# Layer 1's token shift: blended rows projected once, in place of two projections

## The reference

```python
shifted = jnp.pad(hidden, ((0, 0), (1, 0), (0, 0)))[:, :-1]
k_in = hidden * time_mix_key + shifted * (1 - time_mix_key)
v_in = hidden * time_mix_value + shifted * (1 - time_mix_value)
r_in = hidden * time_mix_receptance + shifted * (1 - time_mix_receptance)
k = k_in @ Wk
v = v_in @ Wv
r = jax.nn.sigmoid(r_in @ Wr)
rwkv = _wkv(time_decay, time_first, k, v)   # a scan over the 512 tokens
return r * rwkv @ Wo
```

## Time and profile before

| | us |
|---|---|
| median of 3 runs | 2878.58 (2871.51 to 2892.12) |
| the profiled execution | 2878.1 |
| its span, first to last instruction | 2876.1 |
| granted TensorE clock, mean share of full speed | 0.976 |

### The profile page before, as it was taken

How to read it: one execution, slowest core, us unless ns; L and a number is a source line. 1 busy time by engine, 2 the same in 40 slices (tenths; PEclk the granted TensorE clock), 3 DMA queues, 4 the chain that set the end, 5 groups by cost and what they waited for, 6 DMA issues and landing times. The chain is left out here.

```text
span 2876.1 us, 53577 instructions
## 1 busy us (share of the span) xinstructions
PE 2699.7 (94%) x17974; PEld 1985.7 (69%) x17974; DVE 2295.8 (80%) x4760; ACT 2019.7 (70%) x4630; POOL 725.7 (25%) x709
## 2 busy tenths in 40 slices
PE   6999898999999999999696999999999999999997
PEld 4777675566666577777474777777777777777776
DVE  5988886556656656566685999999999999999997
ACT  3556554645546454453384899999999999999997
POOL 2211101101101100000342333334343433333342
PEclk9999999999999999999898999999999999999999
DMA  2000001000000000000401223223232323223221
GB/s 61 2 5 16 30 16 56 1 1 1 1 1 1 1 1 1 1 1 1 123 1 39 54 67 80 54 64 82 63 82 63 81 64 81 57 64 84 52 52 45
DMA packets 79763, 111.56 MB, mean 39 GB/s; under 512 B 16197, under 2 KB 32776, under 8 KB 79496
## 3 DMA queue, kind: packets, MB, share of 16 engines
q1 hardware_dynamic: 75522, 105.77, 15.1%
q10 hardware_dynamic: 3974, 2.37, 0.3%
HBM read 34.43 MB, written 6.55 MB: 14 GB/s over the span
## 5 line engine op out<-in xcount | busy, mean ns | idle before, releaser
L75 PE MATMUL banks<-lower 128*128 128x128 f32 (+2 forms) x2688 | 480.4, 359 | 1.4 <-DMA lower<-in_L_w2T 0.8
L75 PEld LDWEIGHTS banks<-lower 128*128 128x128 f32 (+1 forms) x2688 | 316.7, 198 | 162.7 <-issue 161.9
L79 PE MATMUL banks<-ident,scratch 128*128 128x128 f32 x2432 | 397.9, 274 | 17.6 <-DVE scratch L83 12.7
L3343 DVE CUSTOM_DVE_ANT_0 scratch<-scratch,tb,coef 128x512 f32<-128x512 f32 (+3 forms) x512 | 399.2, 815 | 0.8 <-ACT scratch L3428 0.8
L79 PEld LDWEIGHTS banks<-ident,scratch 128*128 128x128 f32 x2432 | 293.8, 142 | 118.8 <-issue 102.5
L75 PE MATMUL banks<-scratch 128*128 128x256 f32 (+3 forms) x1088 | 356.0, 432 | 8.9 <-ACT scratch L3024 8.9
L75 PEld LDWEIGHTS banks<-n,pt 128*128 128x128 f32 x2560 | 310.9, 192 | 56.2 <-ACT pt L3450 43.6
L75 PE MATMUL banks<-n,pt 128*128 128x128 f32 x2560 | 344.5, 278 | 4.4 <-ACT moe L3469 4.3
L83 DVE SCALAR_TENSOR_TENSOR scratch<-scratch,tb 128x512 f32<-128x512 f32 (+3 forms) x512 | 344.7, 693 | 0.0
L3514 POOL TENSOR_TENSOR normed<-normed,aT 128x512 f32<-128x512 f32 x128 | 174.0, 1359 | 570.2 <-DVE normed L3304 485.1
L3438 ACT ACTIVATE scratch<-scratch,mn 128x512 f32<-128x512 f32 (+3 forms) x512 | 285.4, 564 | 0.0
(11 more groups left out here) (432 smaller groups left out, 5137.6 us busy)
## 6 DMA issues: line engine op xcount, KB each, us to landing
scratch<-normed SPq DMA_DIRECT2D x512, 128.0 KB, 2.4
tb<-head_rows SPq DMA_DIRECT2D x16, 512.0 KB, 7.5
tb<-head_rows SPq DMA_DIRECT2D x32, 256.0 KB, 7.2
turn<-head_turns SPq DMA_DIRECT2D x32, 128.0 KB, 3.5
xs<-in_x SPq DMA_DIRECT2D x8, 256.0 KB
head_turns<-loads SPq DMA_DIRECT2D x8, 256.0 KB, 2.5
head_turns<-rotation SPq DMA_DIRECT2D x8, 256.0 KB, 2.5
w<-in_L_Wqk SPq DMA_DIRECT2D x8, 256.0 KB, 3.2
```

The lines of the kernel that those rows point to most:

```text
L75: return self.T.matmul(out, lhsT, rhs, start=start, stop=stop, skip_group_check=True)
L79: return self.T.matmul(out, in_, self.ident[0:n, 0:n], start=start, stop=True, is_transpose=True, skip_group_check=True)
L3343: x = V.tensor_tensor_reduce(y, y, view(hd["tb"][:, e, 2, i * P + 127:i * P + 128], [[-1, n]]), k.coef[:, h:h + 1], 3e38, ALU.add, ALU.min ...
```

## The change

`rw_now` and `rw_before` are no longer made: the plain weights `rw` are kept into layer 1. For each projection ScalarE writes (1 - time_mix) times the shifted rows into one of two buffers (the halves of `hT`), VectorE adds time_mix times the rows, in place, and TensorE multiplies the blend once by the plain weight. The six blends of a chunk go through the two buffers in the order of `BLENDS`; a copy waits until the projection two turns before has been done. The key projection of the second sequence goes one slot later on TensorE, from -3 to -2. The prologue's list loses its six weight scalings, so that all later steps of it move six places forward. The counts `l0_prod` and `l0_back` of layer 0 are used again, with a base.

```diff
@@ ahead_dve
         k.made_step(k.ts(k.rest[:, :], k.rp[:, 2:5], -1.0, 1.0, ALU.mult, ALU.add))
         yield
-        for i in range(3):
-            k.made_step(k.ts(k.rw_now[:, i, :], k.rw[:, i, :], k.rp[:, 2 + i:3 + i]))
-            yield
         k.next_made()
-        for i in range(3):
-            k.made_step(k.ts(k.rw_before[:, i, :], k.rw[:, i, :], k.rest[:, i:i + 1]))
-            yield
@@ layer1_prepare
+        k.l1_past, k.l1_blend = k.l0_prod.again(), k.l0_back.again()
+        k.blend = [k.hT[:, j * S:(j + 1) * S] for j in range(2)]
@@
+    BLENDS = ((1, 0), (0, 0), (0, 1), (1, 1), (2, 0), (2, 1))
+
+    def l1_blend_of(self, i, c, b):
+        return 6 * c + self.BLENDS.index((i, b))
@@ l1_pe
         def project(i, c, b):
-            k.l1_emptied_of(T, b, "open", c, b)
-            if c < 2:
-                T.wait_ge(k.pool.sem, k.l1_made)
-            to = take(b)
-            k.mm(to, k.rw_now[:, i, :], k.nT1[c % 2][:, b, 1:1 + S], stop=False)
-            filled(k.mm(to, k.rw_before[:, i, :], k.nT1[c % 2][:, b, 0:S], start=False), b, i, c, b)
+            n = k.l1_blend_of(i, c, b)
+            k.after(T, k.l1_blend, n + 1)
+            filled(k.mm(take(b), k.rw[:, i, :], k.blend[n % 2]), b, i, c, b)
@@
-            for c in due(-3):
+            for c in due(-2):
                 project(0, c, 1)
@@ l1_dve
+        def blend(i, c, b):
+            n = k.l1_blend_of(i, c, b)
+            k.l1_emptied_of(V, b, "open", c, b)
+            k.after(V, k.l1_past, n + 1)
+            k.stt(k.blend[n % 2], k.nT1[c % 2][:, b, 1:1 + S], k.rp[:, 2 + i:3 + i], k.blend[n % 2],
+                  ALU.mult, ALU.add).then_inc(*k.l1_blend.up())
@@
         for s, due in k.l1_slots():
+            for c in due(-7):
+                blend(1, c, 0)
+            for c in due(-5):
+                blend(0, c, 0)
+            for c in due(-3):
+                blend(0, c, 1)
+            for c in due(0):
+                blend(1, c, 1)
+            for c in due(6):
+                blend(2, c, 0)
+            for c in due(7):
+                blend(2, c, 1)
@@ l1_act
+        def past(i, c, b):
+            n = k.l1_blend_of(i, c, b)
+            k.l1_emptied_of(A, b, "open", c, b)
+            if c < 2:
+                A.wait_ge(k.pool.sem, k.l1_made)
+            if n >= 2:
+                c0, (i0, b0) = (n - 2) // 6, k.BLENDS[(n - 2) % 6]
+                k.l1_filled_by(A, b0, i0, c0, b0)
+            A.activation(k.blend[n % 2], k.nT1[c % 2][:, b, 0:S], ACT.Identity,
+                         scale=k.rest[:, i:i + 1]).then_inc(*k.l1_past.up())
@@
             for c in due(-7):
                 open_copy(c, 0)
+                past(1, c, 0)
             if 0 <= s - 2 < k.UNITS1:
                 silu(s - 2, 1)
+            for c in due(-5):
+                past(0, c, 0)
+            for c in due(0):
+                past(1, c, 1)
+            for c in due(6):
+                past(2, c, 0)
+            for c in due(7):
+                past(2, c, 1)
...
             for c in due(-3):
                 open_copy(c, 1)
+                past(0, c, 1)
```

More of the change, by code:

```diff
@@ L169, in ahead_layer1 @@
         k.rwo, k.rp, k.td = k.sb("rwo", [D, D]), k.sb("rp", [D, 5]), k.sb("td", [D, 1])
-        k.rw_now, k.rw_before = k.sb("rw_now", [D, 3, D]), k.sb("rw_before", [D, 3, D])
+        k.rw, k.rw_before, k.rest = k.sb("rw", [D, 3, D]), k.sb("rw_before", [D, 3, D]), k.sb("rest", [D, 3])
     def ahead_layer3(self):
         k = self
-        k.rw, k.rest = k.sb("rw", [D, 3, D]), k.sb("rest", [D, 3])
         k.noise = k.sb("noise", [D, 2, D])
@@ L1904, in layer2_prepare @@
             k.gv2.append(row[:, 0:B * 72].rearrange("p (b a h c) -> p b a h c", b=B, a=4, h=2))
-        k.pool2 = k.shaped(k.rw_now.rearrange("p i d -> p (i d)")[:, 0:B * 128], (B, 2, 64))
+        k.pool2 = k.shaped(k.rw.rearrange("p i d -> p (i d)")[:, 0:B * 128], (B, 2, 64))
         small = k.rw_before.rearrange("p i d -> p (i d)")
```

## The result

The changed kernel takes 2842.88 us (median of 6 runs, 2834.84 to 2852.71), the kernel before beside it 2886.97 us (6 runs). The ratio is 0.9862, with a 95% interval of 0.9844 to 0.9880: 1.4% faster, where 0.6% had been forecast and the range ended at 2848. The profiled execution took 2836.55 us with a span of 2834.9, against 2878.1 and 2876.1 before.

A forecast was written before the change was run, and what follows sets the result against it. TensorE was taken to set layer 1's pace; -18.1 - 1.0 + 0 + 1.1 + 0.5 = -17.5 us gave a predicted 2861 us (-0.6%), chance 0.62, range 2848 to 2880 (within: 0.91).

The forecast's parts named there:

- What leaves TensorE in layer 1, and its cover: Layer 1: 21 second products of 0.86 us leave, 18.1 us saved; added copies (16.3 us) and blends (16.6 us) stay hidden.
- the slack of the experts' chain: Layer 1 slots: 3.5 us between `up` halves, 1.4 filled, 2.1 left; a blend and the shorter projection leave 0.5 us.
- Rival (a): Layer 1: TensorE reaches each projection before its blend, 1.57 us each, net +17 us: 2895, slower; chance 0.06.
- Rival (c): Layer 1: freed TensorE room is worth nothing, pace set by SiLU and product: 2878 us; chance 0.05.
- The stall near slot 69: Chunk 3, slots 66 to 69: a blend delays VectorE's unbroken run, TensorE waits; 1.1 us lost, bounds 0 and 1.3.
- The start of layer 1: First projections wait for copy, moments and blend, partly at half clock; 0.5 us lost, bounds 0 and 3.
- The blends beside GpSimd: Layer 1: a blend meeting a GpSimd operation could double; expected in two or three of 24, mattering only on slot 67.
- The rest of that list: Layer 0: remaining list steps, including five sines and two logarithms, run two slots earlier; zero, bounds -2.5 and +2.5 us.
- Layer 2 and 3 follow in order behind the experts: Layers 2 and 3: they start as much earlier as layer 1's experts end; no further gain counted.
- Rival (b): Clock: displaced work meets two to four more slowdowns, or layer 1's start takes its 3 us: about 2868; chance 0.15.
- Rival (d): More than counted: layer 0's shift falls well, or a half-speed stretch goes: 2853 us; chance 0.12.
- the 1.0 counted: Prologue: six weight scalings leave VectorE ahead of the first window's maximum; 1.0 us saved, bounds 0 and 1.3.

The follow-up runs named there:

- three empty steps: Changed kernel with three empty steps in the prologue's list, so later steps move forward one slot, not two: 2848.78 us, 0.9880 of the kernel before.
- second profile: Both kernels run and profiled once more, unchanged: kernel before 2884.52 us, ratio 1.0016; changed kernel 2844.41 us, ratio 0.9875.
- the padded one: Kernel before with 80 tiny matmuls (160 instructions) added to TensorE's stream at the start of layer 3: 2872.37 us, 0.9963 of the kernel before.
- the one padded in layer 3: Changed kernel with 48 tiny matmuls (96 instructions) added to TensorE's stream at the start of layer 3: 2852.94 us, 0.9891 of the kernel before.

## Why the prediction was wrong

**What leaves TensorE in layer 1, and its cover: right.** The sum for this layer was -18.1 + 1.1 + 0.5 = -16.5 us. Measured: -18.4 and -15.6 in the two pairs of profiles, and -17.2 in the profile with three empty steps, whose half-speed time (14 us) is the kernel before's. The copy is 0.713 us for 0.68, the blend 0.737 for 0.69, both hidden as argued from the slack of the experts' chain. Doubling the copies cost nothing beyond the clock, doubling the blends 5 us and more of 18: the cover was there, and for the blends it is nearly used up. Rival (a), the exposed hand-over, would have shown in TensorE's waits: of 24 projections only two at the start waited for a blend, 4.3 us together, as the prediction said. Rival (c) falls with the same numbers: what left TensorE left the layer's time, although its weight loads are busy for 285 of 454 us. The rule of the Trainium skill on the weight loads' share ("Perfetto Trace Analysis", Identifying the Most-Contended Engine) would have left room here that was not there.

**The stall near slot 69: right in place, less in size.** 0.72 us for 1.1.

**The start of layer 1: right in order, off by 0.5 to 1 us.** The order came out as worked out: the moments stand ahead of the blend, and the first projection waits for it,

```profile
479.26 2.08 PE L75 MATMUL banks<-hT,rw 128*128 128x512 f32 x2 [3.20 <-DVE hT L83]
```

From the `w1` load's issue (470.84) to the first `up` at 485.62 it is 14.8 us, in the second profile 15.6 and with three empty steps 14.9, where the two profiles before have 15.3 and 15.5: nothing to half a microsecond gained, for 0.5 lost. But the earlier trace rows had the experts' start held back by the landing of `w2`, and I took that for a floor; no wait for DMA is left there: all of the layer, its loads too, starts earlier. A row that names the last to arrive gives a floor only from the issue of that load, not as a fixed time.

**The blends beside GpSimd: did not happen.** Two or three were expected to double. The longest of the 24 took 0.750 us (row above). In the kernel with doubled blends four did meet one, and took 2.49. (Two readings behind the sum were loose, without changing it: the 0.69 us of the earlier trace rows are products of L1480, where the addition of 910.99 has a median of 0.68 in the trace; and 283.51 + 16.6 is 300 and not 301.)

**The failed step: "The rest of that list runs three steps to a slot, thus two slots earlier through layer 0 ... I take zero for all this, bounds -2.5 ... and +2.5."** It was -6.8 us. The bound counted table loads, 1.28 us each. What moved was where TensorE waits: a sine that stood in a slot with a GELU made ScalarE's copy late for the transposes, twice, up to 1.87 us; steps of VectorE's own in another slot made `o` late by 1.5; and 6.8 us of half speed stood behind two of these waits. Idle time is 4.9 of the 7.8 us gained there, the clock 2.9. The first was to be seen before: the chain of the step (copy of L1139 behind L505, with the wait at TensorE). I looked at the one sine of slot 28 and took it for all five. Why the clock fell behind the wait of 1.87 us in the two profiles of the kernel before and not in the padded one stays open.

**The second failed step: "Layer 2 and 3 follow in order behind the experts and start as much earlier."** They did start earlier, and ended earlier still: -5.3 and -11.8 us in layer 2, -7.8 and -10.6 in the heads. In layer 2 the program is the same and the length goes with the time at half speed. The layer by windows in, in order, the changed kernel (422.3 us with 38 at half speed in its two profiles and in the one padded in layer 3), the kernel before (second profile), the changed kernel with blends twice; the clock is the last but two:

```profile
937.40:1359.70 422.30, 390.67 (x3229) 296.01 (x3228) 254.68 (x490) 198.22 (x331) 23.39 (x33) 0.96 0.00 1
```

```profile
965.60:1399.80 434.20, 404.58 (x3230) 308.18 (x3228) 254.36 (x491) 198.29 (x331) 23.39 (x33) 0.92 0.00 1
```

```profile
949.60:1385.40 435.80, 409.05 (x3230) 308.26 (x3228) 254.89 (x489) 198.10 (x331) 23.37 (x33) 0.91 0.01 1
```

VectorE, ScalarE and GpSimd have the same work to 0.6 us; TensorE alone is longer, by 14 and 18 us. The other profiles fall nearly in line: 425.1 us with 44 us at half speed, 427.6 with 55 to 58, 429.0 with 58, 432.5 with 61, 432.0 with 65, 432.7 and 434.1 with 68, 435.8 with 79. Rival (b) had this mechanism with the wrong sign only: a displacement can also take half-speed stretches away. Whether it does is not the change's doing alone: the same changes with doubled work had 61 and 79 us. That part, some 5 us and more, I count as not owned by the change. What starts such a stretch in layer 2 was not tried, so that the cause of this part stays open.

In layer 3 the cause is shown by the padding both ways, with the heads' waits and transfers beside it: the change took 48 matmuls and their weight loads out of TensorE's stream, and so moved the fetches of the following code away from the row transfers. That padding of TensorE's stream alone moves them says that they are fetches of its stream; the records of the queue do not name an engine.

**Rival (d)** named two of the three things that the sum lacked, a shift in layer 0 that falls well or a half-speed stretch that goes, at 2853 and a chance of 0.12. It had the direction; its 8 us beyond the sum were too few, and it had nothing for the heads.

**The sum, made up afterwards from these profiles:** -17 in layer 1, -8 on the way to it, -8 to -11 in the heads, and -5 to -12 from the clock in layer 2: 38 to 48, measured 41.2 and 45.8 in the two pairs of profiles. Since its terms are read from the same profiles, that they add up is no test of them. The range was too narrow for the same reason: its lower end, 2848, allowed 13 us beyond the sum for the list and the clock together and nothing for the heads, while outside layer 1 the time fell by 22 us more than the 1.0 counted, in the first pair of profiles.

## What to carry to other kernels

When an edit changes the number of steps in a list that is spread over slots, price every step that moves by what stands in its new and its old slot on its engine, not by its own duration: here a sine beside a GELU and VectorE's steps beside the attention's made TensorE wait 5 us, and the number of table loads told nothing. When an edit changes the number of instructions of an engine with a long unrolled stream, allow for the fetches of its code falling elsewhere, in both directions (here 8 to 11 us of 1465), and keep that apart from what the edit gives: padding both kernels tells. Part of this kernel's gain is such luck, and the next edit may lose it.

## What the runs showed of the hardware

- Row transfers of 128 KB took 2.4 us (median) with no instruction fetch under way and 2.7 to 2.9 us with one, up to 4.1; three in one place took 3.8 (median).
- A VectorE blend (two inputs in SBUF) that started 0.4 us behind a GpSimd addition of 2.33 us took 2.49 us, to 0.55 us past the addition's end, four times; the blend that had started 0.26 us ahead of the addition took 0.73. That fits the Trainium skill ("SBUF — State Buffer", SBUF: two separate sides), by which the pair of ports is held for a whole instruction and the loser waits.
- A switch of ScalarE's tables cost its own 1.28 us and nothing behind it: load at 302.31, GELU at 303.61. The Trainium skill ("ScalarE: Activation LUTs", What ACT_TABLE_LOAD costs) gives some 2.66 us for a switch with the drain; the rows here do not show that part.
- After a wait of 1.87 us the granted clock was 0.50 for 3.4 us, and four matmuls took 3.46 us for 1.88. In another profile the same instructions had the same wait and the clock stayed at 1.00.
